# Row maxima of a quad in five units, merged transfers, barring rows filled from memory, three homes for keys and queries, new instruction lists

## The reference

```python
def attn(x, Wq, Wk, Wv, Wo, gamma, beta):        # 16 heads of 64
    q, k, v = (einsum('bsd,hde->bhse', x, W) for W in (Wq, Wk, Wv))
    scores = einsum('bhse,bhte->bhst', q, k)
    scores = where(causal, scores / sqrt(64), -inf)
    out = einsum('bhst,bhte->bhse', softmax(scores), v)
    y = x + heads(out) @ Wo
    return (y - mean(y)) * rsqrt(var(y) + 1e-3) * gamma + beta

def ffn(x, gate_w, gate_up_w, down_w):           # 32 experts of width 64, best 8 of each token
    top_w, top_idx = top_k(softmax(x @ gate_w.T), 8)
    comb = weights of the 8, divided by their sum, 0 for the other experts
    return sum over e of (u_e * silu(g_e)) @ down_w[e].T * comb[:, e]    # g_e, u_e = x @ gate_up_w[e].T

x = x + attn(_layernorm(x), ...)
x = x + ffn(_layernorm(x), ...)
```

## Time and profile before

| | us |
|---|---|
| median of three runs | 1753.68 |
| runs | 1750.70 to 1754.48 |
| the profiled execution | 1747.59 |
| its span | 1745.7 |
| one trip of the loop (from one `add_experts`, L1237, at 679.9 us to the next but three at 1097.5 us, by four) | 104.4 |

### The profile page before, as it was taken

The page is one execution under the profiler, slowest core; times in us unless marked ns, Lnnn a source line. Parts: engine busy times, 40 slices in busy tenths (PEclk is TensorE's granted clock), DMA queues, the critical chain, the costliest instruction groups (busy, mean ns, idle before and its releaser), DMA issues.

```text
span 1745.7 us, 56980 instructions
## 1 busy us (share of the span) xinstructions
PE 1633.9 (94%) x21209; PEld 1113.7 (64%) x21209; DVE 1462.4 (84%) x4484; ACT 1404.4 (80%) x2364; POOL 1403.9 (80%) x1164
## 2 busy tenths in 40 slices
PE   3799999999999999999999999999999999999868
PEld 1366766666666666666666666666676666667655
DVE  7999889797887978879797887979889797887757
ACT  2799888797887879788797888879788787888752
POOL 4477997888879788887888979788897888889880
PEclk9999999999999999999999999999999999999999
DMA  5554554646455464544646454473645546435423
GB/s 181 128 122 106 145 136 123 166 106 158 104 132 129 106 178 110 142 115 115 174 106 159 110 140 124 104 186 95 158 117 133 139 106 165 123 109 138 112 79 105
DMA packets 219444, 226.26 MB, mean 130 GB/s; under 512 B 27041, under 2 KB 185249, under 8 KB 218913
## 3 DMA queue, kind: packets, MB, share of 16 engines
q1 hardware_dynamic: 219168, 222.61, 49.8%
HBM read 82.53 MB, written 5.24 MB: 50 GB/s over the span
## 4 chain that ended last, share of the span: by engine, by line
PE 61%; SPq 8%; DVE 8%; DMA 6%; POOL 6%; issue 5%; ACT 5%; POOLq 0%; ACTq 0%; DVEq 0%
PE bank_r L389 15%; PE bank_s L389 12%; PE bank_v L389 8%; PE bank_g L389 8%; PE bank_u L389 8%; PE bank_x L389 7%; SPq L321 3%; POOL p_lo L1497 2%; DMA expert_room<-comb_rows 2%; SPq L335 2%; SPq L311 1%; SPq L312 1%; POOL expert_room L1512 1%; DMA xt<-in_x 1%; SPq L310 1%
## 5 line engine op out<-in xcount | busy, mean ns | idle before, releaser
L1497 POOL TENSOR_TENSOR p_lo<-p,p_hi 128x1280 f16<-128x1280 f32 x256 | 674.7, 2636 | 149.0 <-ACT p_hi L786 148.2
L848 ACT ACTIVATE p<-bank_s,back 128x512 f32<-128x512 f32 (+1 forms) x768 | 461.4, 615 | 61.9 <-PE bank_s L389 53.8
L389 PE MATMUL bank_s<-score_ops 128*128 128x62 f16 (+10 forms) x4096 | 405.6, 233 | 20.6 <-DMA score_ops<-rowmaxT 15.3
L389 PEld LDWEIGHTS bank_s<-score_ops 128*128 128x128 f16 x4096 | 278.1, 97 | 192.5 <-issue 46.8
L1512 POOL TENSOR_TENSOR expert_room<-expert_room 128x512 f32<-128x512 f32 x240 | 304.4, 1275 | 34.7 <-DMA expert_room<-comb_rows 17.4
L786 ACT ACTIVATE p_hi<-p 128x1280 f16<-128x1280 f32 x256 | 324.6, 1268 | 7.8 <-PE bank_r L389 2.2
L1516 POOL TENSOR_TENSOR halves<-expert_room,halves 128x512 f16<-128x512 f32 x240 | 276.4, 1162 | 29.0 <-ACT halves L786 27.3
L1124 DVE CUSTOM_DVE_ANT_0 max_junk<-bank_r,mask 128x384 f16<-128x384 f32 (+3 forms) x523 | 232.1, 474 | 36.6 <-PE bank_g L389 16.3
L389 PE MATMUL bank_x<-w_hi,halves 128*128 128x128 f16 x1920 | 199.1, 220 | 2.0 <-POOL halves L1516 2.0
L786 ACT ACTIVATE halves<-expert_room 128x512 f16<-128x512 f32 x240 | 150.1, 625 | 44.8 <-POOL expert_room L1512 32.2
L389 PE MATMUL bank_x<-w_lo,halves 128*128 128x128 f16 x960 | 173.2, 220 | 0.0
(11 more groups left out here) (298 smaller groups left out, 5015.4 us busy)
## 6 DMA issues: line engine op xcount, KB each, us to landing
score_ops<-nat SPq DMA_DIRECT2D x256, 256.0 KB, 3.8
score_ops<-nat SPq DMA_DIRECT2D x512, 128.0 KB, 3.6
expert_room<-comb_rows SPq DMA_DIRECT2D x480, 128.0 KB, 3.0
xt<-in_x SPq DMA_DIRECT2D x16, 256.0 KB, 3.5
xb<-in_x SPq DMA_DIRECT2D x16, 256.0 KB, 4.1
score_ops<-rowmaxT SPq DMA_DIRECT2D x256, 2.0 KB
out_y<-expert_room SPq DMA_DIRECT2D x16, 256.0 KB, 3.4
score_ops<-comb_rows SPq DMA_DIRECT2D x32, 128.0 KB, 3.0
```

The lines of the kernel that those rows point to most:

```text
L389: return pe.matmul(dst, lhsT, rhs, start=start, stop=stop, skip_group_check=shared)
L848: act.activation(p32[:, h % P_SLOTS, at:at + cols], bank[score_bank(h, u)][:, 0:cols], ACT.Exp, scale=back[:, SC_SCORE:SC_SCORE + 1]).then ...
L1497: pool.tensor_tensor(p_lo[:, slot, :], p32[:, slot, :], p_hi[:, slot, :], ALU.subtract).then_inc(p_lo_done, 1)
```

## The change

- The row maxima of a quad (two pairs) are made in five units in place of two times three; the two blocks of 256 columns, one of each pair, now share a bank. The multiplications and the reductions are the same.
- `nat` has three homes in place of two.
- `place_max` uses two transfers in place of four, `keep_weights` one in place of four, `spread_weights` one in place of two. For this the two experts of a unit are interleaved by partition (the host lays `gate_up` and `down` out accordingly) and `comb` is stored with the expert index outermost.
- The barring rows are loaded from memory into each slot by two transfers (`fill_rows`), in place of one load into the last slot and GpSimd's copies.
- Of the 11 parts of the weights, the last seven get their low part from GpSimd (`rest_late`); ScalarE scales the source in place for it first.
- `weigh_last` moves from VectorE to GpSimd.
- The instruction lists of all five engines are written anew.

```diff
-MAX_CHUNKS = ((3,), (0, 2), (1,))
-MAX_UNITS = len(MAX_CHUNKS)
+MAX_BLOCKS = (((0, 3, 0),), ((0, 0, 0), (0, 2, 128)), ((1, 3, 0),), ((1, 0, 0), (1, 2, 128)), ((0, 1, 0), (1, 1, 256)))
+MAX_UNITS = len(MAX_BLOCKS)
+HOMES_QK = 3
...
-        nat = sb("nat", [P, 2, 4, S], F16)
+        nat = sb("nat", [P, HOMES_QK, 4, S], F16)
...
+            def fill_rows(slot):
+                sp.dma_start(score_ops[E:P, 1:4, slot], key_rows_c).then_inc(rows_filled[slot], 16)
+                sp.dma_start(QB[E:P, slot], query_rows_c).then_inc(rows_filled[slot], 16)
...
             def place_max(m, g):
                 wait(sp, score_mm, UNITS * 2 * (m * PAIRS + 2 * g + 1 - SLOTS + 1))
+                if m == 0:
+                    for slot in range(2 * g, min(2 * g + 2, SLOTS)):
+                        sp.wait_ge(rows_filled[slot], 32)
...
-                    for part in range(2):
-                        at = 16 * k + 8 * part
-                        sp.dma_start(home[part:part + 1], rowmaxT[at:at + 8, :]).then_inc(max_placed[g], 16)
+                    sp.dma_start(home, rowmaxT[16 * k:16 * k + 16, :]).then_inc(max_placed[g], 16)
...
-                for c in range(C):
-                    sp.dma_start(comb_rows[:, c * P:c * P + P], combT[c * NE:c * NE + NE, :]).then_inc(comb_stored, 16)
+                sp.dma_start(comb_rows.rearrange("e (c p) -> (e c) p", c=C), combT).then_inc(comb_stored, 16)
...
-                for e in range(2):
-                    sp.dma_start(weighed(p, j)[ED * e:ED * e + ED, :],
-                                 comb_rows[2 * j + e:2 * j + e + 1, :].to_broadcast([ED, S])).then_inc(spread_sem(p, j), 16)
+                both = comb_rows[2 * j:2 * j + 2].rearrange("a (b s) -> b a s", b=1)
+                sp.dma_start(weighed(p, j), both.to_broadcast([ED, 2, S])).then_inc(spread_sem(p, j), 16)
...
+            fill_rows(0); fill_rows(1); load_xb(0); fill_rows(2); load_x(1); place_qk(0, 0); fill_rows(3)
...
                 halve(part)
+                if part >= EARLY:
+                    w = SPLIT[part][0]
+                    act.activation(source(part), source(part), ACT.Copy, scale=w_scale[:, w:w + 1]).then_inc(late_scaled, 1)
...
                 if w == 0:
-                    wait(act, placed[(q - 2) % PAIRS], 96 * (m + 1) if q >= 2 else 96 * m)
-                    wait(act, max_mm, MAX_UNITS * (m * PAIRS + q - 1))
-                copy(nat[:, q % 2, (K_HI, Q_HI)[w], :], bank[b][:, :]).then_inc(proj_hi, 1)
+                    before = m * PAIRS + q - HOMES_QK
+                    if before >= 0:
+                        act.wait_ge(placed[before % PAIRS], 96 * (before // PAIRS + 1))
+                        act.wait_ge(max_mm, MAX_UNITS * (before // 2 + 1))
+                copy(nat[:, home_of(m, q), (K_HI, Q_HI)[w], :], bank[b][:, :]).then_inc(proj_hi, 1)
...
+            def rest_late(part):
+                w, at, cols = SPLIT[part]
+                pool.wait_ge(w_hi_done, part + 1)
+                pool.wait_ge(late_scaled, part - EARLY + 1)
+                pool.tensor_tensor(wl(w, at, cols), source(part), wh(w, at, cols), ALU.subtract).then_inc(late_lo_done, 1)
...
+            def weigh_last(p, j):
+                pool.wait_ge(su_done, p * EP + j + 1)
+                pool.wait_ge(last_spread[j], 16)
+                pool.tensor_tensor(weighed(p, j), weighed(p, j), unit(p, j), ALU.mult).then_inc(last_weighed, 1)
...
-            for side in (KB0, KB1, KB2, QB):
-                rows = side[E:P].rearrange("p a b s -> p (a b) s")
-                pool.tensor_copy(rows[:, 0:2 * SLOTS - 1, :], rows[:, 2 * SLOTS - 1:2 * SLOTS, :].to_broadcast([E, 2 * SLOTS - 1, S])).then_inc(rows_filled, 1)
```

More of the change, by code:

```diff
@@ L775, in _ @@
[L775 to L779 removed]
+            turn_h(0, V); project(0, 0, R0); project(0, 1, G); project(0, 2, R1); max_scores(0, 0, 0, U, V)
@@ new lines, in _ @@
+            gate_product(0, 4, V); max_scores(1, 3, 4, G, U); scores(1, 10, 1); up_product(0, 3, R0)
+            turn_heads(1, 3, R1); values(2, 0, G); gate_product(0, 5, U); times_v(1, 8, V); project(2, 2, R0)
+            scores(1, 10, 2); down_product(0, 0); turn_maxima(1, 3, V); times_wo(1, 1, R1); scores(1, 11, 0)
+            times_v(1, 9, V); max_scores(2, 0, 0, G, U); values(2, 1, R0); scores(1, 11, 1); max_scores(2, 0, 1, R1, G)
+            up_product(0, 4, U); scores(1, 11, 2); project(2, 3, R0); scores(1, 12, 0); up_product(0, 5, R1)
@@ new lines, in _ @@
+            times_v(1, 12, R1); scores(1, 14, 2); project(2, 5, U); gate_product(0, 8, G); scores(1, 15, 0)
+            turn_maxima(2, 0, R0); times_wo(1, 2, R1); times_v(1, 13, G); max_scores(2, 1, 0, V, R0); scores(1, 15, 1)
+            gate_product(0, 9, U); down_product(0, 4); max_scores(2, 1, 1, R1, R0); turn_heads(1, 6, G)
+            gate_product(0, 10, V); scores(1, 15, 2); up_product(0, 8, U); down_product(0, 5); scores(2, 0, 0)
+            project(2, 6, U); times_v(1, 14, R1); project(2, 7, R0); scores(2, 0, 1); up_product(0, 9, V)
@@ new lines, in _ @@
+            project(2, 8, G); down_product(0, 6); scores(2, 0, 2); times_v(1, 15, V); max_scores(2, 1, 2, G, U)
+            up_product(0, 10, R0); project(2, 9, V); turn_heads(1, 7, R1); scores(2, 1, 0); scores(2, 1, 1)
+            down_product(0, 7); max_scores(2, 1, 3, R0, U); max_scores(2, 1, 4, G, V); scores(2, 1, 2)
+            times_wo(1, 3, R1); down_product(0, 8); gate_product(0, 11, R0); gate_product(0, 12, G); scores(2, 2, 0)
+            times_v(2, 0, R1); down_product(0, 9); up_product(0, 11, R0); turn_maxima(2, 1, U); down_product(0, 10)
@@ new lines, in _ @@
+            up_product(13, 0, V); times_v(14, 8, R1); turn_weights(13); scores(14, 10, 1); scores(14, 10, 2)
+            up_product(13, 1, R0); times_v(14, 9, V); turn_heads(14, 3, U); max_scores(14, 3, 4, R1, G)
+            scores(14, 11, 0); gate_product(13, 2, V); project(15, 0, R0); values(15, 0, U); project(15, 1, R1)
+            up_product(13, 2, V); gate_product(13, 3, R0); scores(14, 11, 1); up_product(13, 3, V); times_wo(14, 1, U)
+            gate_product(13, 4, R1); turn_maxima(14, 3, R0); max_scores(15, 0, 0, V, G); scores(14, 11, 2)
@@ new lines, in _ @@
+            down_product(13, 2); times_v(14, 11, R1); scores(14, 14, 0); scores(14, 14, 1); gate_product(13, 7, G)
+            max_scores(15, 0, 4, V, R0); project(15, 4, U); scores(14, 14, 2); project(15, 5, R1); times_v(14, 12, V)
+            down_product(13, 3); scores(14, 15, 0); scores(14, 15, 1); turn_maxima(15, 0, R0); up_product(13, 7, V)
+            gate_product(13, 8, U); max_scores(15, 1, 0, R0, R1); gate_product(13, 9, V); times_v(14, 13, G)
+            scores(14, 15, 2); turn_heads(14, 5, R0); down_product(13, 4); project(15, 6, R1)
@@ new lines, in _ @@
+            up_product(13, 11, V); max_scores(15, 1, 4, U, R1); turn_heads(14, 7, R0); gate_product(13, 11, G)
+            scores(15, 2, 2); down_product(13, 7); scores(15, 3, 0); times_wo(14, 3, R0); times_v(15, 0, G)
+            scores(15, 3, 1); max_scores(15, 2, 0, U, V); gate_product(13, 12, R1); scores(15, 3, 2)
+            down_product(13, 8); turn_maxima(15, 1, R0); project(15, 10, G); gate_product(13, 13, U); times_v(15, 1, R0)
+            up_product(13, 12, V); down_product(13, 9); up_product(13, 13, R1); gate_product(13, 14, G)
```

1229 lines of the change are left out of this document (586 added, 643 removed).

## The result

The changed kernel takes 1696.42 us (median of 4 runs, 1695.44 to 1698.83) against 1752.19 us of the kernel before (4 runs): a ratio of 0.9688, interval 0.9662 to 0.9715. I had forecast 1734, with a range of 1711 to 1751; the sign was right, the size was not. The profiled executions are 1698.8 and 1747.6 us, 48.8 apart, and that difference is what the traces can explain.

What follows compares the result with a forecast made beforehand. PE was taken as the bound: its unchanged work plus 111.8 us of standing still. Start -11, loop -8 and end 0 sum to -19, so 1728.6 us profiled, 1734 as the median; range 1711 to 1751.

Steps and rivals of the forecast that it cites:

- The start: Before the first scores: without GpSimd's copies VectorE's slowed instructions run at full speed; -11 us, range -15 to -5.
- four rows: PE's largest waits in the profile before: maxima transfers 15.3 us, `divide` 10.2, `v_low` 6.2, experts' weights 4.4.
- The loop: The 12 trips: the maxima wait goes, -14 us, new bank waits add 6; -8 us, between -39 and +5.
- this wait goes, 12 x 1.2 = 14 us: In the loop, fewer transfers ahead of the scores bring the maxima 3.3 us earlier, ending PE's wait for them.
- the floor of 100.85 us a trip: PE's work in a loop trip of 104.4 us, taken as unchanged, leaving 3.55 us idle.
- the rival of 1712: All the loop's waits go: start -11, loop -31, giving 1712 us; chance 0.18.
- new reuses of banks: In the loop's new lists, close reuses of a bank hold PE: +0.5 us a trip, +6 us.
- the loop's own bound: Loop's low end: besides the maxima wait, all other recurring waits go, 25 us more; -39 us.
- the first rival: All the loop's waits go, as five units free banks (80 in place of 96): 1712 us; chance 0.18.
- The end: Last products moved from VectorE to GpSimd bring nothing, as PE is full there: 0, between -1 and +3 us.
- All the loop's waits go: Loop rival: freed banks and new lists make `divide` and `v_low` come in time; loop -31, 1712 us; chance 0.18.
- A slower kernel: Rival: the new lists hold PE at its banks in the loop, +19 us, 1762 us in all; chance 0.10.

Runs made afterwards that it cites:

- b_rows: Kernel before with the barring rows loaded by ten transfers, GpSimd's four copies gone, lists otherwise as before: 1744.87 us, ratio 0.9969.
- b_rows_homes: Kernel before with barring rows by transfers and the third home, maxima still in four transfers: 1737.11 us, ratio 0.9935.
- b_parts: Kernel before, old lists and three units a pair, with barring rows by transfers, all merged transfers and the third home: 1698.45 us, ratio 0.9702.
- b_rows_copies: Kernel before with barring rows by transfers, GpSimd still making four copies of the same size into unneeded room: 1753.15 us, ratio 1.0025.
- b_max: Kernel before with the maxima in two transfers in place of four, nothing else: 1711.41 us, ratio 0.977.
- a_ahead2: Changed kernel with two swaps in SP's list: first quad's maxima ahead of the third pair's transfers, second quad's ahead of the next input's load: 1683.78 us, ratio 0.9612.
- a_four: Changed kernel with its transfers unmerged again (maxima four, storing four, spreading two a unit): 1775.53 us, ratio 1.0135.

## Why the prediction was wrong

*The start, -11 forecast, -10.2 measured: the cause right, the closeness of the number in part luck.* The copies do hold up the two slow kinds of instruction, and the first scores came when forecast. But I wrote that the third home brings 0, since ScalarE isn't waited for in four rows of PE's list. By `b_rows` and `b_rows_homes` it carries 10.5 of 14.1 us of the start on the old lists, its effect on the clock included: it was the change's own transfers that made a home scarce. The changed kernel's 10.2 is less than these 14.1, a loss that I hadn't foreseen either. In its start the granted clock is low where that of `b_parts` is full, the first of these rows against the second:

```profile
47.00:66.00 19.00, 15.93 (x127) 8.57 (x126) 15.39 (x61) 17.18 (x25) 13.12 (x12) 0.73 0.90 194
```

```profile
47.00:66.00 19.00, 14.04 (x166) 7.83 (x165) 18.79 (x78) 17.64 (x30) 9.42 (x10) 1.00 0.92 192
```

At 0.73 the stretch is partly at 1.2 and partly at 2.4 GHz, and PE is longer busy with fewer instructions. Whether that is the whole of the 3.5 us to `b_parts` wasn't tried: the late low parts on GpSimd, ScalarE's extra passes and the new lists never ran apart.

*The port lock.* By the Trainium skill, page "SBUF — State Buffer", section "SBUF: two separate sides", a VectorE instruction in a two-port mode, or with two SBUF inputs beside a GpSimd instruction that reads SBUF, is blocked for the whole of a GpSimd instruction. The trace agrees: the copies' and the stalled instructions' ends in `b_rows_copies` are at most 0.03 us apart. That the new work on GpSimd adds nothing of the kind was not tested alone. The end, with 16 new products on GpSimd, came out as forecast; the start, with the low parts, is 3.5 us behind `b_parts`.

*The loop, -8 forecast, -38.5 measured: the failed step.* It is the sizing "Of 3.3 us earlier only 1.55 + 0.7 are needed: this wait goes, 12 x 1.2 = 14 us". The mechanism, transfers in front of the scores, is the right one, and `b_max` shows it alone; its size is not 14 but 34.7 us over the trips (38 in the whole time). Three things were missed. First, I counted one engine's wait row. The same late queue also held VectorE at the input and through it PE at `v_lo` (6.2 us), a row that I had put among the waits that stay. Second, I took PE's busy time for work "which stays the same". The work stays, but the busy time is more than the work: products of 512 columns start 0.21 or 0.22 us apart and are each drawn 0.38 us long, as in this timeline of the changed kernel:

```profile
42.74 0.38 PE L393 MATMUL bank_g<-w_hi,hT 128*128 128x512 f16 x1
42.95 0.38 PE L393 MATMUL bank_g<-w_lo,hT 128*128 128x512 f16 x1
43.17 0.38 PE L393 MATMUL bank_g<-w_hi,hT 128*128 128x512 f16 x1
```

A pause of up to 0.16 us ahead of a product therefore shows as no idle time at all, and of a longer one 0.16 us is missing. The trips at the lower clock are in the busy time too. So the floor of 100.85 us a trip, and with it the rival of 1712 that gave my low end, was no floor: the changed kernel's trips hold 99.1 us of busy time, and `a_ahead2` makes whole trips in 100.20. Third, I added 0.5 us a trip for new reuses of banks, from a look at two places in the new lists. PE's waits for `v_lo` and `o` are 2.2 us together in the whole span of the changed kernel, so those reuses hold PE up hardly at all.

Two readings were loose. The four rows are "3.3 of the 3.55 us a trip" in no count: over the 13 trips they are 35.0 us, 2.7 a trip, and over the four trips of the earlier trace rows 12.4, 3.1 a trip. And the loop's own bound, 14 + 25 = 39, holds the measured 38.5; but the rival that was to be this case was priced at 31 without a reason, and the range was cut at its 1711.

*That the wait for the maxima goes, under 3 us in the span.* Wrong for the changed kernel (15.7 us), right for `b_max`. In both lists the third pair's transfers stand in front of the first quad's maxima. In the new ones the scores follow closer: on average over the loop 5.8 us after `rowmaxT` is ready in the first quad, in place of 7.4, and 5.7 in place of 7.5 in the second, where the next input's load now stands in front. PE then stands 0.6 and 0.7 us there, before 1.2 us in the first quad alone. `a_ahead2` takes it away by order alone.

*The five units and the new lists.* I expected banks to matter in the first rival. On the old lists five units cost 18 us. What units, lists and the work moved to GpSimd do together is the difference of two ratios, 0.9688 (0.9662 to 0.9715) for the changed kernel and 0.9702 (0.9676 to 0.9728) for `b_parts`: -2 us, between about -9 and +4, no difference that these runs can tell. How it is shared among them stays open, since the new lists were run with five units alone.

*The end, 0 forecast and 0 measured* (124.98 us both), with the last products on GpSimd. The kernels with the old lists have 123.0 to 126.3 us there, so a gain or loss of 1 us would not show.

*The rivals.* "All the loop's waits go" was nearest in size, but not what happened: 28.1 us of idle time stay in the 13 trips, and the wait for the maxima is the longest of them. Its price of 31 us was too small. A slower kernel exists, `a_four`, but its wait is for the queue, not for banks.

## What to carry to other kernels

Ask of a full queue not only who waits for its entry but who waits for each entry behind it, and whose wait hides behind theirs. Here halving the few transfers just ahead of PE's next step brought all that the merging of 27 brought, and their place in the list was worth 12.6 us more. A busy time made of overlapping, modelled ends is not work: compare the starts of like instructions, and the granted clock of like trips, before taking it for a floor. A part that is idle in the profile of before (the third home) can carry a change that loads something else (the rows).

## What was not expected of the hardware

- GpSimd's copy of 64x4608 holds up even VectorE instructions of one or two elements to its end (3.40, 3.88 and 3.84 us in place of 0.17, beside copies of 4.02); around each change from one copy to the next one gets through.
- The granted clock fell to its lower level three times in 13 trips before, with PE busy for 97% of them, and never in `b_max`; such a trip has 1.3 to 1.7 us more of PE's busy time.
- A transfer issue blocks ScalarE as it does SP: two issues took 1.30 us and ScalarE was idle for 1.48.
- Two transfers of a few rows from SBUF to memory were issued in 0.77 us, two into `score_ops` in 1.41.
